# An edge stage whose sums are added by TensorE's identity product and ScalarE's copy instead of VectorE

## The chip, the core and the metric

One NeuronCore of a Trainium2 chip runs one program. The metric is the device time of one execution in microseconds (us). TensorE (PE) multiplies matrices into PSUM, VectorE (DVE) and ScalarE (ACT) work on SBUF and PSUM, GpSimd (POOL) here issues the gathers, SyncE (SP) the plain transfers. Each engine has an instruction stream of its own, handled in order; a wait on a semaphore holds what stands behind it in the same stream.

## The reference

A graph attention layer on 3125 nodes and 53125 edges (sorted by destination) is followed by a mixture of eight experts. Only the attention's edge part matters here:

```
qi = q[dst];  kj = k[src];  vj = v[src]
alpha = sum(qi * kj, -1) / sqrt(D)                 # 4 heads of 64
m     = segment_max(alpha, dst)
ex    = exp(alpha - m[dst])
denom = segment_sum(ex, dst)
out   = segment_sum(ex / denom[dst] * vj, dst)
```

## The kernel before

The program has four stages: `project` (key, value tables), `attend` (the edge stage), `mlp` and `experts`. The change is all in `attend`.

`attend` walks over 232 **steps** (STEPS); a step is 256 edges, two tiles of 128 (LT), that all belong to one block of 128 destination nodes. Eight steps are a **chunk** (CP), four chunks a **round** (CR, RING = 32 steps). `walk` writes the first round out, runs the following ones in a hardware loop, and writes out the rest with the tail of ADD_LAG = 17 places. Every engine has its own `at(i, j)` per place; j is the place in the round.

What a step does, by engine, with j the place:

- POOL (L657) gathers the rows of k and v of both tiles by an indirect DMA each into `ring`. It waits until the product of 8 steps before and the sum of 24 steps before are done.
- PE `expand` (L742) makes the queries of the edges by a one-hot product into one of four `psQ`; it first loads the block's number from `brow` into a register (L738) and waits for the product of four steps before.
- DVE multiplies them with the keys (`prod`, L947), then reduces to `alpha` (L987). Between these two it does the pieces of work named below.
- The running maximum of a whole chunk takes a chain over the next eight steps, one piece per step: `alm` (L868, DVE), two transpositions (L772, L773, PE), a copy `nrow` (L707, ACT), a scan (L873, DVE), then pieces that go to and fro between PE (`psR`, `psM`: L778, L781, L786, L789, L794, L798) and DVE (L877 to L931). PE's piece j stands in `rest`, behind the sum of the same `rest`. In step 6 ACT computes the weights `exp` into `ring` (L713).
- PV: 14 steps behind (PV_LAG), ACT multiplies the values by the weights in place: 2 tiles x 4 heads = 8 ACTIVATEs of 128x64 (L722). In the tail, from step 232 on, `shared` is true: ACT does tile 0, and DVE tile 1 in one instruction of 128x256 (L957), with its own semaphore s_pvd.
- DVE makes the one-hot matrix `oh` (L965). 16 steps behind, PE sums with it: four passes of 260 columns into `psA[b % 2]` (L765).
- 17 steps behind, DVE adds `psA` to the block's row of `acc` in SBUF (L981); the block's number comes from `brow` by a register load (L940). Once per chunk DVE first rescales that row by `fac` (L1005); the addition of the chunk's first step waits for it (s_resc).

PE runs `expand(j)` and then `rest(j - 1)`, in which the sum (of step j - 17) comes first and the chain's piece second. ACT's `at` in the order of the code: `idx` for POOL (L685, step 1), chain pieces (L707 in step 0, L710 and L713 in step 6), PV. DVE's: product, chain piece 0, in the tail PV, `oh`, chain piece 1, step 6's build of the one-hot (L834), the addition, chain piece 2, reduction, in step 0 the rescaling.

Of the kernel before, what the change touches and what calls it, by code (L numbers as in the profile page):

```python
# [24 lines left out]
ALU = mybir.AluOpType  # L25
ACT = mybir.ActivationFunctionType
# [6 lines left out]
NB, BP = 25, 128  # L33
# [4 lines left out]
LT = 2  # L38
# [3 lines left out]
STEPS = TILES + NB - 1  # L42
CP = 8
# [3 lines left out]
CR = 4  # L47
RING = CR * CP
R = H * W
HW_ = D + 1  # L50
HALFW = H * HW_
# [3 lines left out]
PV_LAG = CP + 6  # L55
SUM_LAG = CP + 8
# [447 lines left out]
def attend(nc, ctx, io, keep):  # L504

    c = ExitStack()
    with c:
# [82 lines left out]
        def live(i, j, fresh, lag=0):  # L590

            if fresh:
                return j >= lag
            return not isinstance(i, int) or RING * i + j - lag < STEPS

        def staged(i, j, fresh):

            return live(i, j - j % CP, fresh, CP)

        def shared(i, j):  # L600

            return isinstance(i, int) and RING * i + j >= STEPS

        @block.sync
        def _(sp):
# [59 lines left out]
        @block.scalar  # L665
        def _(act):
            def project_out(t):

                act.wait_ge(s_qp, t + 1)
                if t >= 2:  # L670
                    act.wait_ge(s_qlo, t - 1)
                    act.wait_ge(s_reso[t % 2], 16 * (t // 2))
                nc.scalar.activation(qst[:, t % 2, :], psA[t % NA][:, :], ACT.Copy).then_inc(s_qres, 1)
                act.wait_ge(s_qres, t + 1)
                nc.scalar.activation(q3[:, 0, t, :], qst[:, t % 2, 0:HID], ACT.Copy).then_inc(s_qhi, 1)
                nc.scalar.activation(acc[:, t, 0:HID].rearrange("p (k n) -> p k n", k=KC),
                                     iotaF[:, :].unsqueeze(1).broadcast_to([P, KC, P]), ACT.Copy, scale=0.0).then_inc(s_zero, 1)
                act.wait_ge(s_qr1, t + 1)
                nc.scalar.activation(q3[:, 1, t, :], qst[:, t % 2, 0:HID], ACT.Copy).then_inc(s_qmid, 1)

            def places(cc, par, fresh):

                if not fresh:
                    act.wait_ge(s_kv[CP - 1], 16 * LT * (cc - 1))
                nc.scalar.activation(idx[:, par, :], keep["srcI"][:, bass.ds(W * cc, W)], ACT.Copy).then_inc(s_idx, 1)  # L685

            def starts(m, par):

                nc.scalar.activation(stc[:, par, :, :], keep["startN"][:, bass.ds(W * m, W)].unsqueeze(1).broadcast_to([P, H, W]),
                                     ACT.Copy).then_inc(s_stc, 1)  # L690

            places(0, 0, True)
            for t in range(QEARLY):
                project_out(t)

            def at(i, j, fresh):
                if j % CP == 1 and live(i, j - 1, fresh, -CP):
                    places(CR * i + j // CP + 1, (j // CP + 1) % 2, fresh and j < CP)
                if fresh and QEARLY + j < NB:
                    project_out(QEARLY + j)  # L700
                m = CR * i + j // CP - 1
                jj = j % CP
                if staged(i, j, fresh):
                    if jj == 0:
                        starts(m, (j // CP - 1) % 2)
                        act.wait_ge(s_mp, NT * m + T_IN)
                        nc.scalar.activation(nrow[:, 0:P], psM[0:R, P:2 * P], ACT.Copy).then_inc(s_nrow, 1)  # L707
                    if jj == 6:
                        act.wait_ge(s_mv, NV * m + V_FMIN)
                        nc.scalar.activation(fx[:, :], fm[:, :], ACT.Exp, scale=SCALE).then_inc(s_fx, 1)  # L710
                        act.wait_ge(s_mv, NV * m + V_DIFF)
                        out = ring[:, :, (j // CP - 1) % CR, :].rearrange("p w (h e) -> p h w e", h=H)[:, :, :, D]
                        nc.scalar.activation(out, dif[:, :, :], ACT.Exp, scale=SCALE).then_inc(s_exp, 1)  # L713
                if live(i, j, fresh, PV_LAG):

                    sj = (j - PV_LAG) % RING
                    bc = CR * i + (j - PV_LAG) // CP
                    act.wait_ge(s_exp, bc + 1)
                    for k in range(LT if shared(i, j) is False else 1):
                        for h in range(H):  # L720
                            row = ring[:, LT * (sj % CP) + k, sj // CP, h * HW_:(h + 1) * HW_]
                            last = nc.scalar.activation(row[:, 0:D], row[:, 0:D], ACT.Copy, scale=row[:, D:HW_])  # L722
                    last.then_inc(s_pv, 1)

            walk(act, at)

        @block.tensor
        def _(pe):
# [18 lines left out]
            def rest(i, j, fresh):  # L747
# [4 lines left out]
                if live(i, j, fresh, SUM_LAG):  # L752

                    b = RING * i + j - SUM_LAG
                    sj = (j - SUM_LAG) % RING
                    pe.wait_ge(s_pv, b + 1)
                    if isinstance(b, int) and b >= STEPS - PV_LAG:
                        pe.wait_ge(s_pvd, b - (STEPS - PV_LAG) + 1)
                    pe.wait_ge(s_oh, b + 1)
                    if fresh and j == SUM_LAG:  # L760
                        pe.wait_ge(s_qres, NB)
                    if not (fresh and j < SUM_LAG + NA):
                        pe.wait_ge(s_acc, b - NA + 1)
                    for k in range(LT):
                        last = nc.tensor.matmul(psA[sj % NA][0:BP, 0:HALFW], oh[:, sj % NO, k, :],  # L765
                                                ring[:, LT * (sj % CP) + k, sj // CP, :], start=(k == 0), stop=(k == LT - 1))
                    last.then_inc(s_agg, 1)
                if jj == 0:
                    pe.wait_ge(s_mv, NV * m + V_ALPHA)
                    pe.wait_ge(s_stc, m + 1)  # L770
# [54 lines left out]
        def _(dve):  # L825
# [108 lines left out]
            def at(i, j, fresh):  # L934
                step = RING * i + j
                cc, q, jj = CR * i + j // CP, j // CP, j % CP
                now = staged(i, j, fresh)
                if live(i, j, fresh, ADD_LAG):
                    b = step - ADD_LAG
                    blk = nc.vector.value_load(brow[0:1, bass.ds(b, 1)], min_val=0, max_val=NB - 1)  # L940
                if live(i, j, fresh):

                    dve.wait_ge(s_kv[jj], 16 * LT * (cc + 1))
# [25 lines left out]
                    maximum(i, j, 1)  # L969
                if jj == 6 and live(i, j, fresh, -CP):  # L970
                    build(2 * i + (q + 1) // 2, cc + 1, (q + 1) % CR)
                if live(i, j, fresh, ADD_LAG):

                    sj = (j - ADD_LAG) % RING
                    dve.wait_ge(s_agg, b + 1)
                    if not (fresh and j < ADD_LAG + 1):
                        dve.wait_ge(s_acc, b)
                    if sj % CP == 0:
                        dve.wait_ge(s_resc, CR * i + (j - ADD_LAG) // CP + 1)
                    row = acc[:, bass.ds(blk, 1), :].rearrange("p a d -> p (a d)")  # L980
                    nc.vector.tensor_tensor(row, row, psA[sj % NA][0:BP, 0:HALFW], ALU.add).then_inc(s_acc, 1)  # L981
                if now:
                    maximum(i, j, 2)
                if live(i, j, fresh):
# [837 lines left out]
```

## Time and profile before

| | us |
|---|---|
| median of three runs | 1486.68 (1482.07 to 1489.24) |
| the profiled execution | 1487.41, span 1485.6 |
| PE, DVE, ACT, POOL busy | 1259.2, 1099.3, 780.8, 836.5 |
| last addition of the edge stage | at 752 |

The granted TensorE clock is 0.96 on average. Busy time counts neither waits nor the sequencers' register loads. In the timelines a start and a length stand first; lengths overlap, so what an instruction costs is read from start to start. "[0.30 <-issue]" is idle time just before, with what ended it; "issue" is idle time for which the profile shows no other engine's work.

### The profile page before, as it was taken

Reading aid. Unit: us, or ns where it says so; the run is one execution under the profiler, and the core shown is the slowest. Engines: PE = TensorE matmul, PEld = TensorE weight load, DVE = VectorE, ACT = ScalarE, POOL = GpSimd, SP = SyncE. Lnnn points to the kernel's source line nnn. Section 1 sums busy time; section 2 is a strip of 40 time slices with the busy share of each in tenths; the row PEclk is TensorE's granted clock in tenths of the full one; section 3 lists DMA queues with packets and bytes.
Section 4 is the critical chain, followed back from the end, with each engine's and each line's share of the span. In section 5 each row is a group of like instructions: output and inputs, shape, how many; then the busy total and the mean of one; then the engine's idle time right before and its main releaser. Section 6 shows DMA issues by size and latency. Waiting matters only on the chain. (4 is left out here: it accounts for less than half of the span.)

```text
span 1485.6 us, 29780 instructions
## 1 busy us (share of the span) xinstructions
PE 1259.2 (85%) x7188; PEld 985.3 (66%) x7189; DVE 1099.3 (74%) x2825; ACT 780.8 (53%) x2538; POOL 836.5 (56%) x874
## 2 busy tenths in 40 slices
PE   4899877777877777677759999868899999999998
PEld 2434555454555545455537777667899999999997
DVE  4747899898998989899955555367856656566565
ACT  1255888786876778677732222233334434444343
POOL 2146677777777777777310111036566757566564
PEclk9999999999999999999979999968999999999999
DMA  5367777777777777777340111142110010100000
GB/s 186 124 219 221 211 226 224 223 225 222 217 226 226 223 217 225 229 223 220 109 131 4 51 53 53 33 139 65 40 37 19 1 53 0 35 18 0 18 1 17
DMA packets 83555, 184.24 MB, mean 124 GB/s; under 512 B 11611, under 2 KB 46262, under 8 KB 83454
## 3 DMA queue, kind: packets, MB, share of 16 engines
q0 software_dynamic: 37632, 124.28, 29.4%
q1 hardware_dynamic: 44438, 57.57, 11.9%
q10 hardware_dynamic: 1384, 1.32, 0.3%
q8 instruction: 31, 0.51, 0.1%
q14 instruction: 70, 0.57, 0.1%
HBM read 165.93 MB, written 17.18 MB: 123 GB/s over the span
## 5 line engine op out<-in xcount | busy, mean ns | idle before, releaser
L657 POOL DMA_INDIRECT ring<-kv_rows,idx x464 | 478.7, 1032 | 174.7 <-issue 132.3
L722 ACT ACTIVATE ring<-ring 128x64 f32<-128x64 f32 x1800 | 438.3, 336 | 0.9
L1540 ACT ACTIVATE hf<-psF,k_scT 128x320 f32<-128x320 f32 x320 | 197.8, 618 | 221.4 <-PE psF L1573 212.2
L742 PE MATMUL psQ<-k_q,ohT 128*128 x1392 | 206.1, 282 | 93.5 <-issue 93.4
L765 PE MATMUL psA<-ring,oh 128*128 128x260 f32 x928 | 251.4, 395 | 2.7 <-DVE k_acc L981 2.5
L742 PEld LDWEIGHTS psQ<-k_q,ohT 128*128 128x128 bf16 x1392 | 120.5, 98 | 150.3 <-issue 125.8
L1507 POOL TENSOR_TENSOR h2l<-hf,h2h 128x320 fp32r<-128x320 f32 x160 | 148.8, 944 | 111.6 <-DVE h2h L1716 111.6
L947 DVE TENSOR_TENSOR prod<-psQ,ring 128x512 f32<-128x512 f32 x232 | 158.1, 681 | 35.0 <-issue 21.2
L1507 POOL TENSOR_TENSOR h1l<-hf,h1h 128x320 fp32r<-128x320 f32 x160 | 148.5, 950 | 61.5 <-DVE h1h L1716 61.5
L765 PEld LDWEIGHTS psA<-ring,oh 128*128 128x128 f32 x928 | 163.8, 197 | 24.2 <-ACT ring L722 4.1
L987 DVE TENSOR_REDUCE alpha<-prod 128x8 f32<-128x512 f32 x232 | 155.8, 671 | 0.2
L1716 DVE CAST h2h<-hf 128x320 fp32r<-128x320 f32 x160 | 89.8, 577 | 63.3 <-ACT hf L1540 63.3
L1716 DVE CAST h1h<-hf 128x320 fp32r<-128x320 f32 x160 | 82.5, 521 | 58.5 <-ACT hf L1540 58.4
L1573 PE MATMUL psO<-wh,h2l 128*128 128x256 f32 x400 | 108.8, 293 | 9.1 <-DVE o L1705 8.3
L1705 DVE SCALAR_TENSOR_TENSOR o<-psO,wt,o 128x256 f32<-128x256 f32 x200 | 92.5, 479 | 30.7 <-PE psO L1573 29.2
L1573 PE MATMUL psO<-wl,h2h 128*128 128x256 f32 x400 | 105.6, 285 | 0.0
L1573 PE MATMUL psF<-xh,wl 128*128 128x320 f32 x320 | 101.3, 324 | 0.0
L1573 PE MATMUL psF<-xl,wh 128*128 128x320 f32 x320 | 100.2, 320 | 0.0
L1573 PE MATMUL psF<-h1h,wl 128*128 128x320 f32 x320 | 97.5, 313 | 0.0
L1573 PE MATMUL psF<-h1l,wh 128*128 128x320 f32 x320 | 96.3, 309 | 0.0
L1137 POOL TENSOR_SCALAR ve<-mv 128x5 f32<-128x5 f32 x10 | 3.3, 329 | 164.2 <-DVE mv L1261 99.5
L981 DVE TENSOR_TENSOR k_acc<-k_acc,psA 128x260 f32 x232 | 93.7, 404 | 2.8 <-PE psA L765 1.0
(234 smaller groups left out, 2323.6 us busy)
## 6 DMA issues: line engine op xcount, KB each, us to landing
ohT<-step_destinations SPq DMA_DIRECT2D x29, 512.0 KB, 5.0
ring<-kv_rows,idx POOLq DMA_INDIRECT x464, 3.8
kv_rows<-kvst SPq DMA_DIRECT2D x25, 260.0 KB, 2.1
we<-in_L_ffn_W SPq DMA_DIRECT2D x16, 256.0 KB, 3.1
residual<-qst SPq DMA_DIRECT2D x25, 128.0 KB, 3.5
resin<-residual SPq DMA_DIRECT2D x5, 640.0 KB, 6.6
after_graph_layer<-x SPq DMA_DIRECT2D x5, 640.0 KB, 5.7
xres<-after_graph_layer SPq DMA_DIRECT2D x5, 640.0 KB, 4.4
```

The costliest lines, as they stand in the source:

```text
L657: nc.gpsimd.indirect_dma_start(out=ring[:, LT * (j % CP) + k, j // CP:j // CP + 2, :].rearrange("p t e -> p (t e)"), out_offset=None, in_= ...
L722: last = nc.scalar.activation(row[:, 0:D], row[:, 0:D], ACT.Copy, scale=row[:, D:HW_])
L742: last = nc.tensor.matmul(psQ[j % NQ][:, k * HID:(k + 1) * HID], ohT[par][:, w * P:(w + 1) * P], q3[:, part, bass.ds(blk, 1), :].rearrange ...
L765: last = nc.tensor.matmul(psA[sj % NA][0:BP, 0:HALFW], oh[:, sj % NO, k, :], ring[:, LT * (sj % CP) + k, sj // CP, :], start=(k == 0), sto ...
L947: nc.vector.tensor_tensor(prod[:, j % 2, :].rearrange("p (k d) -> p k d", k=LT), psQ[j % NQ][:, :].rearrange("p (k d) -> p k d", k=LT), ri ...
L981: nc.vector.tensor_tensor(row, row, psA[sj % NA][0:BP, 0:HALFW], ALU.add).then_inc(s_acc, 1)
L987: nc.vector.tensor_reduce(alpha[:, q % 2, :, LT * jj:LT * jj + LT].rearrange("p h w -> p w h"), prod[:, j % 2, :].rearrange("p (k h d) -> ...
L1507: nc.gpsimd.tensor_tensor(low, hf[:, n, 0:b - a], high, ALU.subtract).then_inc(s_rl, 1)
L1540: nc.scalar.activation(hf[:, n, 0:b - a], psF[n][:, 0:b - a], ACT.Relu, bias=scT[:, 2 * layer - 1, col + m:col + m + 1], scale=scT[:, 2 * ...
L1573: mm = nc.tensor.matmul(out, ws(k)[iw], xs(k)[ix], start=(at == 0), stop=(at == len(n) - 1))
L1705: nc.vector.scalar_tensor_tensor(out=o[:, u, :], in0=ps, scalar=wt[:, u, e:e + 1], in1=o[:, u, :], op0=ALU.mult, op1=ALU.add).then_inc(s_c ...
L1716: nc.vector.tensor_copy(high, hf[:, n, 0:b - a]).then_inc(s_rh, 1)
```

## The change

In every step, not only in the tail, `shared` is now true in odd places and false in even ones: in odd ones DVE scales tile 1 and ACT tile 0, in even ones ACT scales both. The addition leaves DVE. PE gets, behind the sum, a register load of the block's number, a wait for the copy of the step before (and, in a chunk's first step, for the rescaling), and a product of the identity with the block's row of `acc`, accumulated into the same `psA`. ACT gets a register load and a copy of `psA` into that row of `acc`, ahead of its chain pieces and PV.

```diff
         def shared(i, j):
-            return isinstance(i, int) and RING * i + j >= STEPS
+            return j % 2 == 1
...
         (ACT, at)
+                if live(i, j, fresh, ADD_LAG):
+                    b = RING * i + j - ADD_LAG
+                    blk = nc.scalar.value_load(brow[0:1, bass.ds(b, 1)], min_val=0, max_val=NB - 1)
+                    act.wait_ge(s_agg, b + 1)
+                    nc.scalar.activation(acc[:, bass.ds(blk, 1), :].rearrange("p a d -> p (a d)"),
+                                         psA[(j - ADD_LAG) % RING % NA][0:BP, 0:HALFW], ACT.Copy).then_inc(s_acc, 1)
...
-                    for k in range(LT if shared(i, j) is False else 1):
+                    for k in range(LT if not shared(i, j) else 1):
...
         (PE, rest)
-                    if isinstance(b, int) and b >= STEPS - PV_LAG:
-                        pe.wait_ge(s_pvd, b - (STEPS - PV_LAG) + 1)
+                    if sj % 2 == (1 - PV_LAG) % 2:
+                        pe.wait_ge(s_pvd, (RING // 2) * i + (j - SUM_LAG) // 2 + 1)
...
                     for k in range(LT):
-                        last = nc.tensor.matmul(psA[sj % NA][0:BP, 0:HALFW], oh[:, sj % NO, k, :],
-                                                ring[:, LT * (sj % CP) + k, sj // CP, :], start=(k == 0), stop=(k == LT - 1))
-                    last.then_inc(s_agg, 1)
+                        nc.tensor.matmul(psA[sj % NA][0:BP, 0:HALFW], oh[:, sj % NO, k, :],
+                                         ring[:, LT * (sj % CP) + k, sj // CP, :], start=(k == 0), stop=False)
+                    blk = nc.tensor.value_load(brow[0:1, bass.ds(b, 1)], min_val=0, max_val=NB - 1)
+                    if not (fresh and j < SUM_LAG + 1):
+                        pe.wait_ge(s_acc, b)
+                    if sj % CP == 0:
+                        pe.wait_ge(s_resc, CR * i + (j - SUM_LAG) // CP + 1)
+                    nc.tensor.matmul(psA[sj % NA][0:BP, 0:HALFW], ident[:, :], acc[:, bass.ds(blk, 1), :].rearrange("p a d -> p (a d)"),
+                                     start=False, stop=True).then_inc(s_agg, 1)
...
         (DVE, at)
-                if live(i, j, fresh, ADD_LAG):
-                    b = step - ADD_LAG
-                    blk = nc.vector.value_load(brow[0:1, bass.ds(b, 1)], min_val=0, max_val=NB - 1)
...
-                if live(i, j, fresh, ADD_LAG):
-
-                    sj = (j - ADD_LAG) % RING
-                    dve.wait_ge(s_agg, b + 1)
-                    if not (fresh and j < ADD_LAG + 1):
-                        dve.wait_ge(s_acc, b)
-                    if sj % CP == 0:
-                        dve.wait_ge(s_resc, CR * i + (j - ADD_LAG) // CP + 1)
-                    row = acc[:, bass.ds(blk, 1), :].rearrange("p a d -> p (a d)")
-                    nc.vector.tensor_tensor(row, row, psA[sj % NA][0:BP, 0:HALFW], ALU.add).then_inc(s_acc, 1)
```

## Rows read from the trace of the kernel before

**Rows 1.** Stretches: start:end, us, busy us (instructions) by engine, clock, DMA share, GB/s.

```profile
185.00:722.00 537.00, 407.79 (x2363) 277.12 (x2361) 498.15 (x1374) 418.05 (x1760) 415.06 (x400) 0.97 0.77 223
```

**Rows 2.** Groups from 185 to 722: line, engine, op, tiles | busy us, mean ns | idle before.

```profile
L657 POOL DMA_INDIRECT ring<-kv_rows,idx x400 | 415.1, 1038 | 121.8 <-issue 96.6 <-PE psA L765 17.4 <-DVE prod L947 6.7
...
L742 PE MATMUL psQ<-k_q,ohT 128*128 x1220 | 180.9, 282 | 89.4 <-issue 89.3
```

**Rows 3.** Timeline of POOL: start us, length us, line, op [idle before].

```profile
409.26 0.95 POOL L657 DMA_INDIRECT ring<-kv_rows,idx  x1 [0.30 <-issue]
...
414.25 1.22 POOL L657 DMA_INDIRECT ring<-kv_rows,idx  x1 [0.30 <-DVE prod L947]
...
422.03 1.66 POOL L657 DMA_INDIRECT ring<-kv_rows,idx  x1 [0.30 <-DVE prod L947]
```

**Rows 4.** Timeline of DVE, step 7 of two rounds, and the loop's end.

```profile
363.27 0.68 DVE L947 TENSOR_TENSOR prod<-psQ,ring 128x512 f32<-128x512 f32 x1
...
449.20 0.69 DVE L947 TENSOR_TENSOR prod<-psQ,ring 128x512 f32<-128x512 f32 x1
...
455.03 0.69 DVE L947 TENSOR_TENSOR prod<-psQ,ring 128x512 f32<-128x512 f32 x1 [3.75 <-issue]
```

**Rows 5.** Timeline of all engines, steps 7, 0 and 1 around a rescaling.

```profile
406.80 0.69 DVE L947 TENSOR_TENSOR prod<-psQ,ring 128x512 f32<-128x512 f32 x1
407.12 0.74 PEld L765 LDWEIGHTS psA<-ring,oh 128*128 128x128 f32 x4
...
407.89 0.75 PEld L742 LDWEIGHTS psQ<-k_q,ohT 128*128 128x128 bf16 x6
...
409.54 0.42 DVE L965 TENSOR_TENSOR oh<-k_iotaF,k_dstR 128x256 f32<-128x256 f32 x1
...
409.77 0.27 PE L772 MATMUL psM<-k_ident,alm 128*64 128x128 f32 x1
...
410.18 0.27 ACT L707 ACTIVATE nrow<-psM 64x128 f32<-64x128 f32 x1 [1.07 <-PE psM L773]
...
410.80 0.42 DVE L1005 TENSOR_TENSOR k_acc<-k_acc,fac 128x260 f32 x1
...
411.39 1.04 PE L765 MATMUL psA<-ring,oh 128*128 128x260 f32 x4
...
411.95 0.40 DVE L873 TENSOR_TENSOR_SCAN F<-nrow,psM 64x128 f32<-64x128 f32 x1
...
412.59 0.41 DVE L981 TENSOR_TENSOR k_acc<-k_acc,psA 128x260 f32 x1
412.92 0.67 DVE L987 TENSOR_REDUCE alpha<-prod 128x8 f32<-128x512 f32 x1
```

**Rows 6.** Timeline of DVE one chunk on, steps 7 and 0.

```profile
426.73 0.69 DVE L947 TENSOR_TENSOR prod<-psQ,ring 128x512 f32<-128x512 f32 x1
...
431.16 0.69 DVE L947 TENSOR_TENSOR prod<-psQ,ring 128x512 f32<-128x512 f32 x1 [2.35 <-DMA ring<-kv_rows,idx]
```

**Rows 7.** Groups of the whole span: the scaling on DVE, copies from PSUM, the sum.

```profile
L957 DVE TENSOR_TENSOR ring<-ring 128x256 f32<-128x256 f32 x14 | 5.8, 413 | 0.7 <-ACT ring L713 0.4 <-issue 0.2
...
L254 ACT ACTIVATE k_acc<-psT 128x256 f32<-128x256 f32 x25 | 9.6, 383 | 61.2 <-PE psT L285 61.2
...
L673 ACT ACTIVATE qst<-psA 128x512 f32<-128x512 f32 x25 | 14.9, 595 | 17.2 <-PE psA L806 16.4 <-DMA residual<-qst 0.7
...
L765 PE MATMUL psA<-ring,oh 128*128 128x260 f32 x928 | 251.4, 395 | 2.7 <-DVE k_acc L981 2.5
```

**Rows 8.** Timeline of ACT in the tail.

```profile
740.40 7.74 ACT L722 ACTIVATE ring<-ring 128x64 f32<-128x64 f32 x32
```

**Rows 9.** Instructions of line L738: duration ns min/median/max.

```profile
L738 PEldq TENSOR_LOAD <-k_brow x203: 296/302/322, 186.6 to 720.8; - x102
```

**Rows 10.** Timeline of PE: a chunk product and the expansion behind it.

```profile
403.15 0.27 PE L794 MATMUL psM<-k_ident,Gm 64*128 64x64 f32 x1
404.05 0.85 PE L742 MATMUL psQ<-k_q,ohT 128*128 x6 [0.63 <-issue]
```

## The prediction

> **What bounds the kernel now.** I read the table of stretches first: the edge stage is the only one that the change touches, and in its steady part (185 to 722 us) VectorE (DVE) is busy 93% of the time, TensorE (PE) 76%, ScalarE (ACT) 78%, GpSimd (POOL) 77% [rows 1]. That invites "DVE is the bound, take work off it". The list of groups says more: POOL's 400 gathers there take 1038 ns each and each is preceded by 0.30 us of idle time, so 400 x 1.342 = 537 us, the whole stretch of 537 us [rows 2]. The timeline of POOL shows it as a chain without a hole: every gather starts 0.30 us after the one before, and what stretches it is that some last 1.14 to 1.66 us instead of 0.95 [rows 3]. A step has two gathers, so a round of 32 steps costs 64 x 1.342 = 85.9 us, and DVE's product of step 7 of a round's last chunk stands at 363.27 and, one round on, at 449.20: 85.9 us [rows 4].
>
> DVE's own pace is faster. From a chunk's product of step 7 at 406.80 to the next at 426.73 are 19.9 us, in a dense row [rows 5, 6]. Four chunks are 79.7 us; at the loop's end DVE loses 3.75 us before its next product [rows 4]; together 83.5 us. The 2.4 us to 85.9 are waits for a gather: "2.35 <-DMA" before the product at 431.16 [rows 6]. So a round has two limits, 85.9 by the gathers and 83.5 by the chain of DVE and PE, and the change works on the second alone. **Making DVE lighter cannot pay more than the gathers allow**; making the chain longer costs from 2.4 us per round on.
>
> **What leaves and what comes, per chunk of 8 steps.** DVE loses eight additions of 0.41 us; by starts they cost 0.33 each (412.59 to 412.92) [rows 5]. It gains four scalings of 128x256; the tail has this instruction 14 times, 0.413 us each [rows 7], so by the same overlap 0.33. Net 8 x 0.33 - 4 x 0.33 = -1.3 us: DVE alone would need 18.6. Its register load for the addition goes too; it lay under the reduction and is worth 0 to 0.1 us each.
>
> ACT loses 16 of 64 scalings per chunk, 0.24 us each by starts (7.74/32) [rows 8], -3.9, and gains eight copies of 128x260 out of PSUM. No such copy is in the trace; 128x256 from PSUM takes 383 ns [rows 7], so 8 x 0.4 = +3.2, up to 0.6 each at the upper end (128x512 takes 595 ns) [rows 7]. ACT is busy 78% and stays there. But its copy stands first in its step, and now two engines wait for it.
>
> PE gains a product of 260 columns in two passes per step. Four such passes take 1.04 us with the overhang of the last, whose own length is 0.39, so they start (1.04 - 0.39)/3 = 0.22 apart [rows 5, 7]: +0.44 us. It also gains a register load. The one that is there shows 302 ns for the load alone [rows 9]; by starts a chunk's product at 403.15 is followed by the expansion at 404.05, 0.9 us later, though where PE had queued work, as behind the sum at 407.12, the expansion's weights load at 407.89 with no gap [rows 5, 10]. The new load stands behind four queued passes (0.88 us), so I take it as hidden, with 0.9 us per step as the other end. The price of a step in PE's instruction stream is then: expansion to sum 0.6, sum 0.88, identity 0.44, chunk product 0.3, and 0.2 of the next register load left over: 2.4 us. DVE's step is 18.6/8 = 2.3. So **PE becomes about equal to DVE, and each wait in front of it counts**.
>
> **The new waits.** PE's product for step b now waits for ACT's copy of b-1, and on the first step of a chunk for DVE's rescaling. What is queued behind it on PE is the scan's transposition of that same slot, and behind that is ACT and DVE. Three stalls per chunk follow. I place them from X, the end of the rescaling (411.22) [rows 5].
>
> First: the transpositions of alm and stc ran at 409.77, before the rescaling, and ACT's nrow was done at 410.45, 0.8 before. Now they stand behind the identity product that waits for X: X + 0.1 + 0.5 (identity) + 0.45 (two transpositions) + 0.3 (nrow) gives the scan at X + 1.45. It ran at 411.95, X + 0.73. Stall 0.7.
>
> Second: ACT's queue has nrow, then the eight scalings of that even step (1.9 us), then the idx copy (0.1), then the copy of the sum. Nrow is done at X + 1.35, so the copy is seen at X + 3.8; PE's next identity product waits for it, and the carry product behind it is done at X + 4.8. DVE would want that (L877) at X + 1.45 + 3 x 0.33 (scan, scaling, one-hot) + 2 x 0.6 (reduction, next product) = X + 3.65. Stall 1.2.
>
> Third: PE's following step starts late for the same reason, and DVE's read of cin meets its product 0.4 late. After that both run at 2.3 to 2.4 and meet again at the next rescaling. Sum: 19.9 - 1.3 + 0.7 + 1.2 + 0.4 = 20.9 us per chunk.
>
> A round: 4 x 20.9 + 3.75 = 87.4 us against 85.9 now, +1.5. With 232/32 = 7.25 rounds, +11 us. Bounds of the stalls: none (the round stays at 85.9, +0), and twice as long (+2.3 per chunk, 96.6 per round, +77); I take the placed ones, since each is a queue order read from the code with durations from rows.
>
> **The tail.** From step 232 on DVE has scaled one tile of two in each step already; now ACT takes both in even steps. The last eight such steps cost ACT 7.74 us for 32 scalings without a gap, 0.97 per step [rows 8]; after, (48 x 0.24 + 8 x 0.4)/8 = 1.84. That is 0.87 more for each of the seven or so steps in which no scan gives it cover: about +6, between +2 and +10. The stages before and after are untouched.
>
> **Sum.** The profiled execution took 1487.4 us (span 1485.6), 0.7 above the median of 1486.7. 1487.4 + 11 + 6 = 1504.4; I say 1505.
>
> **A rule on the port.** Gathers that run beside a DVE instruction with two SBUF inputs (L965 at 409.54) last the usual 0.95 us (the one of 409.26) [rows 3, 5]; the new scaling is of that kind and adds no lengthening by this row. The Trainium skill (SBUF — State Buffer, "SBUF: two separate sides") says that DVE and GpSimd take a shared pair of ports by exclusive lock, in a fast mode of DVE or, against a GpSimd instruction that reads SBUF, with two SBUF inputs, and that GpSimd then cannot write descriptors. By that rule this trace agrees only if a gather does not count as reading SBUF. If it does count, it would speak against this change, and the time is that of the third rival.
>
> **The rivals.**
> 1. The gathers still decide. If the three stalls sum to under about 1.9 us instead of 2.3, the round stays under 85.9: 1487.4 + 0 + 2 to 6 = 1489 to 1494. For: the difference is only 0.4 us in a chunk. Against: the queue orders are strict.
> 2. PE's stream decides. If the new register load is not hidden for 0.3 us or so of each step, PE needs 2.7 per step, a chunk 21.6 plus part of the stalls, some 22: 4 x 22 + 3.75 = 91.8, +5.9 per round, +43, with the tail 1536. At the full 0.9 it would be 3.3 per step, 26 per chunk, +166; the gap-free expansion at 407.89 speaks against that. For: the idle time before expansions, 89 us, is called "issue" [rows 2], so the sequencer does cost time there. It decides from 2.6 us per step on.
> 3. The gathers get longer. Each of 116 new DVE scalings holds a gather back for up to 0.41 us: 16 x 0.41 = 6.6 per round on 85.9, 92.5 per round, +48 at most; half of it 1487 + 24 + 6 = 1517. For: the gathers' lengths do vary, 1038 ns mean over the usual 0.95 us. Against: L965 above.
> 4. Faster. If DVE's lighter load let gathers run at the shortest length, 64 x 1.25 = 80 per round, and the stalls hid, 4 x 18.6 + 3.75 = 78, the round could fall to 80: -5.9 x 7.25 = -43, with the tail 1450; a third of it, some 1478, is likelier. It needs both at once. Nothing on DVE that is removed is known to lengthen a gather.
>
> **How the numbers follow.** The forecast 0.45, own range 1495 to 1520; rival 1 0.22; rival 2 0.20; rival 3 0.05; rival 4 0.08. Half a per cent, 7.4 us, is about what a measurement can tell from no change. Slower by over that: all of 2 and 3, nearly all of the forecast, a little of 1: 0.70. Same: 0.22. Faster: 0.08. The range leaves out rival 4 and the long end of rival 2: 1486 to 1545.
>
> **What would show it.** In the profile after: POOL has waits longer than 0.30 us before its gathers (now it has none), and a round is over 86 us; DVE waits some 0.7 us before L873 on ACT's nrow and 1.2 us before L877 on PE, once per chunk; ACT idles before its copies, waiting for PE; expansions are not over 2.5 us apart outside these places. If POOL still has no hole, rival 1 holds; if PE is never idle but for "issue" and steps are 2.6 or more throughout, rival 2; if gathers' mean is over 1100 ns, rival 3. Wrong altogether would be a stage under 85 us per round.

## The result, and the profile after

The changed kernel takes 1520.16 us (1519.73 to 1527.88), the kernel before in the same comparison 1485.85 (1481.53 to 1489.24): ratio 1.0238, 95% interval 1.0216 to 1.0261. Slower, as forecast, and inside the range; but +34 us by the medians where +18 was forecast, and at the upper end of the 1495 to 1520 that the prediction gave its own mechanism. The profiled execution is the longest of its six, 1527.88 (span 1526.1).

First the stretch of [rows 1] in the kernel after (same columns), then POOL's gathers from 190 to 734 us (in [rows 2] they are those from 185 to 722):

```profile
185.00:722.00 537.00, 472.60 (x2637) 330.69 (x2635) 450.86 (x1209) 372.04 (x1481) 419.27 (x382) 0.98 0.75 214
```

```profile
L657 POOL DMA_INDIRECT ring<-kv_rows,idx x386 | 425.3, 1102 | 119.0 <-issue 99.0 <-PE psA L779 11.3 <-DVE prod L957 4.4
```

DVE is busy 84% of the stretch instead of 93%, ACT 69% instead of 78%, PE 88% instead of 76%: two engines were relieved and the stage got slower. Only 382 gathers fit where 400 did, and they last 1102 ns on average instead of 1038.

What DVE waits for, in the kernel after, 190 to 734 us (us in total, times, longest):

```profile
DVE tails L890 <- PE psR L791: 27.2, 25, 1.8
DVE F L886 <- ACT nrow L714: 23.9, 24, 1.6
DVE prod L957 <- PE psQ L749: 11.9, 4, 3.1
DVE cin L902 <- PE psR L794: 9.6, 22, 0.5
...
DVE prod L957 <- DMA ring<-kv_rows,idx: 0.4, 1, 0.4
```

And the same list for the kernel before, 190 to 707 us:

```profile
DVE prod L947 <- issue: 21.0, 10, 4.1
DVE prod L947 <- DMA ring<-kv_rows,idx: 9.0, 7, 2.4
```

The waits for gathers are gone, and three waits have come, each about once per chunk (22 to 25 times): on ACT's `nrow`, on PE's carry product, on PE's product behind `cin`. These are the three places that were forecast. The timeline of the kernel after around one rescaling shows how the first two come about (start, length, engine, line, idle before):

```profile
427.40 0.43 DVE L1005 TENSOR_TENSOR k_acc<-k_acc,fac 128x260 f32 x1 [0.34 <-issue]
...
428.08 0.70 PE L779 MATMUL psA<-k_acc,k_ident 128*128 x2 [0.29 <-DVE k_acc L1005]
...
428.62 0.27 PE L785 MATMUL psM<-k_ident,alm 128*64 128x128 f32 x1
...
429.04 0.27 ACT L714 ACTIVATE nrow<-psM 64x128 f32<-64x128 f32 x1 [2.39 <-PE psM L786]
...
429.21 2.01 ACT L729 ACTIVATE ring<-ring 128x64 f32<-128x64 f32 x8
429.41 0.41 DVE L886 TENSOR_TENSOR_SCAN F<-nrow,psM 64x128 f32<-64x128 f32 x1 [0.97 <-ACT nrow L714]
...
431.23 0.36 ACT L708 ACTIVATE k_acc<-psA 128x260 f32 x1
...
431.73 0.70 PE L779 MATMUL psA<-k_acc,k_ident 128*128 x2 [0.76 <-ACT k_acc L708]
...
432.37 0.27 PE L791 MATMUL psR<-k_ident,F 64*1 64x64 f32 x2
...
432.67 0.21 DVE L890 COPY tails<-psR 1x64 f32<-1x64 f32 x1 [1.01 <-PE psR L791]
```

The identity product (L779) waits for the rescaling; the transposition L785 stands behind it, `nrow` behind that, and DVE's scan comes 1.6 us after the rescaling's end, where it came 0.7 after it in [rows 5]. Then ACT does eight scalings before its copy (431.23), PE's next identity product waits for the copy, the carry product (L791) stands behind it, and DVE waits 1.01 us.

Where the time lies, from the starts of DVE's products and of the gathers:

| us | before | after | |
|---|---|---|---|
| to the first gather | 88.4 | 91.4 | +3.0 |
| first gather to product of step 31 | 109.3 | 110.5 | +1.2 |
| six rounds, product of step 31 to that of step 223 | 509.0 | 532.1 | +23.1 |
| to the last product (step 231) | 19.4 | 22.8 | +3.4 |
| tail: last product to the first use of the sums | 26.7 | 33.3 | +6.6 |
| rest of the program | 732.7 | 735.9 | +3.2 |

The first and the last line are untouched code; from kernel to kernel of this document the first moves between 88.4 and 91.4 us and the last between 729 and 736, without a change in them, so those 6 us are no part of the change. The stage itself gained 34.3 us in this execution. That it equals the difference of the medians is chance: the profiled executions lie 40.5 us apart, and how much of the 34.3 a median execution has isn't known.

### The profile page after: what moved, and what is told of

Its sections match the earlier page's. It is cut to its first block and busy times, and to the rows that moved or that the text cites. A ratio compares the mean times of both kernels' runs of the same rounds, so it can differ in the third digit from the quotient of the medians.

```text
span 1526.1 us, 31630 instructions
## 1 busy us (share of the span) xinstructions
PE 1362.9 (89%) x7652; PEld 1069.2 (70%) x7653; DVE 1066.3 (70%) x2695; ACT 763.3 (50%) x2363; POOL 861.0 (56%) x874
## 5 line engine op out<-in xcount | busy, mean ns | idle before, releaser
L657 POOL DMA_INDIRECT ring<-kv_rows,idx x464 | 503.4, 1085 | 177.3 <-issue 138.8
L729 ACT ACTIVATE ring<-ring 128x64 f32<-128x64 f32 x1392 | 355.3, 337 | 0.9
L772 PE MATMUL psA<-ring,oh 128*128 128x260 f32 x928 | 247.5, 390 | 1.0 <-ACT ring L729 1.0
L749 PE MATMUL psQ<-k_q,ohT 128*128 x1392 | 201.7, 280 | 37.1 <-issue 35.5
L779 PE MATMUL psA<-k_acc,k_ident 128*128 x464 | 146.4, 398 | 39.1 <-ACT k_acc L708 19.5
L772 PEld LDWEIGHTS psA<-ring,oh 128*128 128x128 f32 x928 | 161.9, 194 | 19.9 <-ACT ring L729 1.4
L708 ACT ACTIVATE k_acc<-psA 128x260 f32 x232 | 88.5, 381 | 121.3 <-PE psA L779 98.9
L779 PEld LDWEIGHTS psA<-k_acc,k_ident 128*128 128x128 f32 x464 | 82.6, 192 | 73.3 <-issue 61.1
L1705 DVE SCALAR_TENSOR_TENSOR o<-psO,wt,o 128x256 f32<-128x256 f32 x200 | 92.5, 479 | 33.3 <-PE psO L1573 31.9
```

The costliest lines, as they stand in the source:

```text
L657: nc.gpsimd.indirect_dma_start(out=ring[:, LT * (j % CP) + k, j // CP:j // CP + 2, :].rearrange("p t e -> p (t e)"), out_offset=None, in_= ...
L749: last = nc.tensor.matmul(psQ[j % NQ][:, k * HID:(k + 1) * HID], ohT[par][:, w * P:(w + 1) * P], q3[:, part, bass.ds(blk, 1), :].rearrange ...
L779: nc.tensor.matmul(psA[sj % NA][0:BP, 0:HALFW], ident[:, :], acc[:, bass.ds(blk, 1), :].rearrange("p a d -> p (a d)"), start=False, stop=T ...
L1705: nc.vector.scalar_tensor_tensor(out=o[:, u, :], in0=ps, scalar=wt[:, u, e:e + 1], in1=o[:, u, :], op0=ALU.mult, op1=ALU.add).then_inc(s_c ...
```

## The experiments

In all of them the six rounds of the table serve as the measure of the stage. e1 to e4 ran on one chip (kernel before 1483.6 us), e5 and e10 to e12 on a second (1482.39), e6 to e9 on a third, of which more below. "After the first" means the last five of the six rounds; the first of them has no end of the hardware loop in it.

**What the gathers allow in the kernel before.** DVE's addition shrunk to 4 of 260 columns (the kernel leaves out the rest of the sums):

```diff
-  nc.vector.tensor_tensor(row, row, psA[sj % NA][0:BP, 0:HALFW], ALU.add)
+  nc.vector.tensor_tensor(row[:, 0:4], row[:, 0:4], psA[sj % NA][0:BP, 0:4], ALU.add)
```

> The kernel before, with DVE's additions cut to 4 of 260 columns (the other columns of the sums are left out); waits and order are unchanged. It asks whether the gathers limit the kernel before. If they do (my theory): DVE's own chunk falls from 19.9 to some 18 us, but a round stays near 85.9 us and the time within 1472 to 1486. Rival, that a gather's shown length is only what the chain of DVE and PE leaves it: a round falls by some 8 to 10 us and the time to 1415 to 1430.

1472.92 us, ratio 0.9907 (0.9872 to 0.9942); six rounds 496.6. The waits and the gathers, 190 to 720 us:

```profile
DVE prod L947 <- DMA ring<-kv_rows,idx: 16.8, 20, 2.4
...
L657 POOL DMA_INDIRECT ring<-kv_rows,idx x397 | 397.4, 1001 | 120.9 <-issue 105.4 <-PE psA L765 8.8 <-DVE prod L947 5.8
```

In the stretch of [rows 1] DVE is busy 467.76 us instead of 498.15. With rounds of 83.6 and 85.8 us that is 72.8 us per round instead of 79.6, 6.8 less; but a round after the first became only 2.2 us shorter, and the waits for gathers grew (16.8 us where the kernel before has 9.0): they are a limit of the kernel before, as expected. But the limit itself moved, from 1038 to 1001 ns a gather. 64 x (1.001 + 0.305) = 83.6 us is the round that it had (82.8 to 85.0 after the first).

**The additions alone.** The whole change but for `shared`, so that ACT scales all tiles except in the tail:

```diff
-  return j % 2 == 1
+  return isinstance(i, int) and RING * i + j >= STEPS
```

> The other half: the additions go to PE and ACT, ACT scales all tiles but in the tail. DVE needs 8 x 0.33 = 2.6 us less per chunk than before, 17.3, with the stalls of 2.8 us 20.1; but ACT has 8 x (8 x 0.24 + 0.4) = 18.6 us per chunk in a loop with PE, and its backlog behind nrow is longer. My theory: 21 to 22.5 us per chunk, 1512 to 1540. Rival, that the extra scaling on DVE and not the copy on ACT makes the changed kernel slow: under 1500.

1502.48 us, 1.0118 (1.0081 to 1.0156); six rounds 520.5. Waits and gathers, 190 to 720 us:

```profile
DVE tails L890 <- PE psR L791: 34.3, 24, 2.0
DVE F L886 <- ACT nrow L714: 25.6, 24, 1.6
DVE prod L957 <- issue: 22.3, 5, 5.1
DVE cin L902 <- PE psR L794: 9.4, 23, 0.5
...
L657 POOL DMA_INDIRECT ring<-kv_rows,idx x392 | 384.2, 980 | 147.3 <-issue 117.5 <-PE psA L779 24.9 <-DVE prod L957 4.0
```

The three waits are there, 69.3 us in 24 chunks, 2.9 per chunk; the gathers are short, and POOL has idle time of 0.376 us before one instead of 0.305: here they wait, and the chain sets the pace. The time lies between the two expectations: the three waits are there, but moving the additions carries only half of the loss.

**The DVE scaling alone.** Kernel before with `shared` as after; the additions stay on DVE.

```diff
-  return isinstance(i, int) and RING * i + j >= STEPS
+  return j % 2 == 1
```

> The kernel before with one half of the change: DVE scales one of four value tiles, the additions stay on DVE. DVE gets 4 x 0.33 = 1.3 us per chunk more. With the gathers' limit of 85.9 us: a round is 4 x 21.2 + 3.75 = 88.6, +2.7, in all with 2 to 3 us for the tail 1504 to 1512. Without such a limit 29 x 1.3 = +38: 1522 to 1526. If the ports are contended, the gathers' mean goes over 1100 ns and DVE waits for them.

1525.76 us, 1.0273 (1.0234 to 1.0312), no better than the whole change, whose interval it overlaps. It is above the 1504 to 1512 expected with a limit by the gathers and in the 1522 to 1526 expected without one; DVE has no wait for a gather that shows. Its six rounds, 543.5, are 11 us longer than those of the whole change. A chunk takes 21.4 us (median), 1.5 more than the 19.9 before: four scalings of 0.37. That gives 4 x 21.4 + 3.75 = 89.4 per round, but a round after the first took 91.0 to 91.9. The missing 2 us stand at the loop's end, timeline of DVE:

```profile
474.28 0.69 DVE L947 TENSOR_TENSOR prod<-psQ,ring 128x512 f32<-128x512 f32 x1 [4.07 <-issue]
...
476.86 0.43 DVE L981 TENSOR_TENSOR k_acc<-k_acc,psA 128x260 f32 x1 [1.43 <-issue]
```

A second gap, before the addition two instructions on, was not there before; the profile calls it "issue" too. What makes it was not found.

**The order on PE.** In three kernels PE's pieces of the scan were put ahead of the sum and the identity product: with the whole change only the two transpositions (e2), with the whole change all pieces (e11), with the additions alone all pieces (e10). The edit in each is a move inside `rest`:

```diff
+                if jj == 0:
+                    ...                    # transpositions of alm and stc
+                if jj == 2:
+                    ...                    # carry product and the later pieces, in e10 and e11
                 if live(i, j, fresh, SUM_LAG):
                     ...                    # sum and identity product
-                if jj == 0:
-                    ...
```

> The changed kernel, with PE's two transpositions of a chunk's step 0 ahead of the sum and the identity product instead of behind them. It takes away the cause of the first stall (nrow waits behind the rescaling) and, since ACT's eight scalings and its copy then start earlier, of the second. My theory: DVE's waits before L886 and before L890, 0.97 and 1.08 us per chunk in the changed kernel, go nearly to zero, a chunk falls from 21.4 to 19.4 to 19.9 us, and the gathers' 85.9 us per round then limit: 1495 to 1506. Without a limit by the gathers it would be 1460 to 1470. Rival, that PE's instruction stream is the bound: 1515 to 1520, no change.

> The whole change with the same order on PE: scan pieces ahead of the sum and the identity product in every step. Theory (the gathers, lengthened by the DVE scaling to 1065 to 1085 ns, then decide): DVE no longer waits before the scan and the tails, the round is 64 x (1.07 + 0.304) = 87.9, as it was with only the transpositions moved: 1503 to 1512. Rival (the DVE scaling does not lengthen gathers, they only follow the chain's pace): they fall back to 1000 to 1040 ns and the round to 83.5 to 86, time 1478 to 1495.

> Additions alone moved (ACT scales as before), and PE's pieces of the scan (transpositions, carry product) stand ahead of the sum and the identity product in every step. With the additions moved and no DVE scaling the gathers lasted 980 ns, so their limit is 64 x (0.980 + 0.304) = 82.2 us per round against 85.9 before. Theory (only the three placed waits held that version back): they go, the chunk falls from 20.8 to 19 to 19.8 us, the round to 80 to 83.5, and the time to 1468 to 1488 with a tail 6 us longer, ratio 0.99 to 1.003. Rival (PE's stream is the next limit once the waits are gone): the chunk stays at 20.3 or over, round 85 to 87, time 1488 to 1500.

| | median us | ratio (95%) | six rounds |
|---|---|---|---|
| whole change | 1520.16 | 1.0238 (1.0216 to 1.0261) | 532.1 |
| e2, transpositions first | 1507.86 | 1.0151 (1.0109 to 1.0193) | 521.5 |
| e11, all pieces first | 1507.81 | 1.0159 (1.0110 to 1.0208) | 521.0 |
| e4, additions alone | 1502.48 | 1.0118 (1.0081 to 1.0156) | 520.5 |
| e10, additions alone, all pieces first | 1489.16 | 1.0024 (0.9998 to 1.0049) | 504.7 |
| kernel before | | | 509.0 |

e10's waits of DVE and its gathers, then those of e11, then e2's, 190 to 720 us:

```profile
DVE prod L957 <- PE psQ L749: 51.7, 75, 3.9
DVE prod L957 <- issue: 22.0, 7, 5.2
...
L657 POOL DMA_INDIRECT ring<-kv_rows,idx x397 | 393.4, 991 | 129.8 <-issue 95.2 <-PE psA L810 19.2 <-DVE prod L957 12.9
```

```profile
DVE prod L957 <- PE psQ L749: 50.2, 80, 3.8
DVE k_acc L1005 <- ACT k_acc L708: 9.6, 24, 1.3
...
L657 POOL DMA_INDIRECT ring<-kv_rows,idx x385 | 413.4, 1074 | 117.3 <-issue 96.0 <-PE psA L810 10.7 <-DVE prod L957 7.3
```

```profile
DVE prod L957 <- DMA ring<-kv_rows,idx: 18.3, 14, 2.9
DVE tails L890 <- PE psR L791: 17.8, 22, 1.6
DVE prod L957 <- PE psQ L749: 14.8, 14, 3.0
...
L657 POOL DMA_INDIRECT ring<-kv_rows,idx x384 | 413.5, 1077 | 117.0 <-issue 93.3 <-PE psA L786 17.4 <-DVE prod L957 5.5
```

The waits before the scan, the tails and `cin` are all gone from e10 and e11, and with them 15.8 and 11.1 us of the six rounds: the queue order on PE was the cause of them, shown in both pairs (each pair lies on two chips, whose kernels before agree within 0.3%). With the transpositions alone ahead, e2, the first of the waits goes and the second stays at 17.8 us of 27.2, where nearly nothing was expected. What is late next differs. In e10 it is PE's expansion (51.7 us in 75 waits): PE's stream is the limit, at 84.1 us per round, between the two expectations, and the time is the kernel before's. In e2 it is the gathers again (18.3 us), with 64 x (1.077 + 0.305) = 88.4 us per round against 88.0 seen after the first. e11 has the same gathers, 64 x (1.074 + 0.305) = 88.3, and 87.5 seen, but DVE's waits there are for PE's expansion (50.2 us) and 1.3 us in all for gathers: PE's stream holds it, at about the gathers' own pace.

The four kernels make a square. Pieces behind instead of ahead: +0.9 points of the ratio without the scaling, +0.8 with it. Scaling on DVE: +1.4 with pieces ahead, +1.2 behind. Each ratio is known to 0.2 to 0.5 points. So of the loss of 2.4 points **about a third (0.8 to 0.9 points) is the order on PE and about half (1.2 to 1.4) the scaling on DVE**, as long as the additions are moved. Where they stay on DVE the same scaling costs 2.7 points (e3, against 2.4 for both): moving the additions costs 1.2 by itself and nothing that shows beside the scaling, so the costs of the two edits don't add up. What is left, e10's 0.2, is no more than a measurement can tell from nothing, and is made of 4 us less in the rounds and 5 us more in the tail (32.0 against 26.7).

**Does the register load on PE cost?** The whole change, the identity product reading row 0 always, without the load of the block's number:

```diff
-  blk = nc.tensor.value_load(brow[0:1, bass.ds(b, 1)], min_val=0, max_val=NB - 1)
...
-  nc.tensor.matmul(..., ident[:, :], acc[:, bass.ds(blk, 1), :].rearrange("p a d -> p (a d)"), ...)
+  nc.tensor.matmul(..., ident[:, :], acc[:, 0, :], ...)
```

> The whole change, but PE's identity product reads row 0 of the accumulator always, so that PE loads no register for it (the sums are then wrong, the work is the same otherwise). Theory (the placed waits and the longer gathers make the time): the register load lay under queued passes, the chunk stays at 21 to 21.5 us, the round at 88 to 89.5, the time within 6 us of the whole change's 1520, ratio to before 1.019 to 1.025. Rival (PE's instruction stream costs): 0.3 us or more of each step comes back, the chunk falls by 1.5 to 2.4 us, the round falls to the gathers' own limit of 87 to 88 us, and the time to 1500 to 1508, ratio 1.010 to 1.015.

1515.11 us, 1.0198 (1.0147 to 1.0249); six rounds 529.3 against 532.1, 0.5 us per round. Its interval takes in the whole change's ratio: 2.8 us in 192 steps, 0.015 a step. The gathers hide a part of it: a chunk without a loop's end fell from 21.4 to 21.1 us, 0.04 a step, while DVE now waits for gathers, 190 to 720 us:

```profile
DVE prod L956 <- DMA ring<-kv_rows,idx: 2.5, 4, 1.4
```

Either way the load is nearly hidden, and the prediction's second rival, which needed 0.3 a step, is out.

**What a DVE instruction does to the gathers.** The additions alone, plus a product of 128x256 on DVE in odd steps, into a tile that nobody reads:

```diff
+  if j % 2 == 1:
+      nc.vector.tensor_tensor(scr[:, :], ring[:, LT * jj, q + 1, 0:HID],
+                              ring[:, LT * jj + 1, q + 1, 0:HID], ALU.mult)
```

> Additions alone moved, as in the version that took 1502, plus a product of two 128x256 SBUF tiles on DVE in odd steps, where the change has its scaling; its result goes to a scratch tile that nobody reads, and nobody waits for it. The chunk gets 4 x 0.33 to 4 x 0.41 = 1.3 to 1.6 us of DVE's time. Theory (any such instruction on DVE lengthens the gathers beside it): gathers' mean goes from 980 to 1030 or more, and the time from 1502 to 1515 to 1530, ratio 1.020 to 1.030. Rival (the lengthening in the whole change came through ACT or PE, not through DVE's product): gathers stay within 15 ns of 980, and the time rises only by DVE's own share, 4 x 1.3 to 1.6 per round in the chain or +35 at most, with the gathers' waits for free slots growing instead.

1507.98 us, 1.0152 (1.0097 to 1.0207), six rounds 522.9. Its gathers, 190 to 720 us:

```profile
L658 POOL DMA_INDIRECT ring<-kv_rows,idx x388 | 406.9, 1049 | 123.9 <-issue 96.6 <-PE psA L780 25.2 <-ACT idx L686 1.8
```

1049 ns against 980 in e4, and 991 in e10 on the same chip: with a DVE instruction more, on which nothing depends, the gathers get longer; the work of ACT and PE is the same as in e4. Not because the dummy stands beside them, though. In the six rounds the gathers exceed 946 ns (their median) by 39 us in all instead of 12 in e4, and 18 of these 27 us fall on one gather per chunk, the one under way when DVE builds `ohT` in step 6, an even step, in which the dummy doesn't run. The dummy moves what DVE does against the gathers; the section on the hardware has the rows.

The time rose by 5 us only, less than the 13 to 28 expected, and by ratio not clear of noise (1.0152 against e4's 1.0118). DVE's waits took up most of the new work (before the scan 16.5 us instead of 25.6, before `cin` none instead of 9.4), and the longer gathers were not yet the limit. The real scaling costs some 18 us. It has the dummy's length on DVE, but PE's sum waits for the scaled tile, and ACT scales less; which of these makes the difference no run shows.

**On the third chip** the same kernels e10, e11 and e12 had run before (as e7, e6, e8), and e9, in which one input of the dummy product comes from PSUM:

```diff
-  nc.vector.tensor_tensor(scr[:, :], ring[:, LT * jj, q + 1, 0:HID],
+  nc.vector.tensor_tensor(scr[:, :], psQ[j % NQ][:, 0:HID],
```

> The changed kernel with all of PE's chain pieces (not only step 0's) ahead of the sum and the identity product of the same place. My theory: DVE's waits before L886, L890 and L902 come from the order on PE, so they fall below 0.3 us per chunk together; DVE's own chunk is then under 19.5 us, and what limits is the gathers, which DVE's scaling lengthens (1071 ns mean with the transpositions first): 64 x (1.07 + 0.30) = 88 us per round, 1500 to 1508. Rival, that PE's instruction stream with its second register load is the bound: 1515 or more, and expansions 2.6 us or more apart.

> The additions moved alone (ACT scales all tiles, as in e4_adds_alone), with PE's chain pieces ahead of the sum in every place. If the stalls of e4 (35.5, 26.6 and 9.6 us of DVE waits) come from the order on PE and the gathers keep their 980 ns without DVE's scaling, a round falls from 87.5 us to the gathers' 64 x 1.284 = 82.2 or to ACT's 4 x 19.5 = 78 plus the loop's end: 1460 to 1480, faster than the kernel before. If ACT's eight scalings behind nrow are the cause of the second wait, L890's wait stays and it is 1490 to 1500.

> e4_adds_alone with one added DVE instruction in odd places, a product of 128x256 of two tiles in SBUF (both in the gathered ring) into a scratch tile that nobody reads. It has the size and the two SBUF inputs of the scaling. If such an instruction holds gathers back, their mean rises from 980 by 50 to 120 ns; if it does not, it stays within 15 ns. Either way DVE's chain gets 4 x 0.33 = 1.3 us per chunk longer: 1520 to 1542 against 1502.

> The same as e8_two_sbuf, but the added instruction reads one tile in PSUM and one in SBUF. If two SBUF inputs are what lengthens gathers, the mean stays within 15 ns of 980 here while it rises in e8; if any DVE time of that length does it, both rise alike. The time is that of e8 or, if gathers matter to it, less: 1515 to 1540.

There the kernel before takes 1647.33 us and a round of e7 109.8 us after the first (84.7 in e10), so that the expected times don't apply; the gathers, 64 x 1.31 = 84 us a round, don't limit it there. The ratios are 1.0169 (1.0109 to 1.0228) for e6, 1.0079 (1.0045 to 1.0114) for e7, 1.0259 (1.0201 to 1.0317) for e8 and 1.0280 (1.0209 to 1.0352) for e9. e6 and e7 keep the order that e11 and e10 have on the second chip, but e8 is e12's kernel, which had 1.0152 there: ratios don't carry over from chip to chip. e8 and e9 are alike in time. The gathers of e8, e9 and, without a dummy, e7, 190 to 720 us:

```profile
L658 POOL DMA_INDIRECT ring<-kv_rows,idx x302 | 317.0, 1050 | 214.1 <-issue 115.5 <-remote 48.9 <-DVE prod L961 26.5
```

```profile
L658 POOL DMA_INDIRECT ring<-kv_rows,idx x302 | 307.7, 1019 | 223.5 <-issue 130.6 <-remote 56.6 <-PE psA L780 31.6
```

```profile
L657 POOL DMA_INDIRECT ring<-kv_rows,idx x310 | 311.7, 1006 | 219.5 <-issue 72.1 <-remote 63.1 <-PE psA L810 62.3
```

With one input in PSUM the gathers last 1019 ns, with both in SBUF 1050, without a dummy 1006; over the whole stage the means are 1028, 1035 and 1004. So the dummy with one PSUM input adds 13 or 24 ns, the one with two SBUF inputs 44 or 31, by the stretch that is taken: a mean over gathers doesn't settle whether the inputs matter (e7 also has the other order on PE, which goes with 11 ns between e4 and e10). The Trainium skill (SBUF — State Buffer, "SBUF: two separate sides") has GpSimd locked out of a port pair shared with DVE. That gathers end at fixed distances behind one DVE instruction, as the last section shows, agrees with it; which of DVE's instructions lock and why there are two distances no run here tells.

## Why the prediction was right, and where its sizes were not

- *The gathers bound the kernel before, the chain the kernel after.* Right: e1 for the first; for the second, 0.4 us of waits for gathers in the kernel after, and 11 us less when the order on PE alone is changed (e11).
- *Three stalls of 0.7, 1.2 and 0.4 us per chunk.* Right in place and sum: 23.9/24 = 1.0, 27.2/25 = 1.1 and 9.6/22 = 0.4, 2.5 against 2.3.
- *DVE needs 18.6 us without the stalls.* The chunk is 21.4 us in the median, without 2.5 that is 18.9. So a chunk was 0.5 us longer than forecast and a round 2.0.
- *A round of 87.4.* Measured 88.7 to 89.8 from the second on, 89.2 on average; 4 x 21.4 + 3.0 = 88.6. The loop's end is now a gap of 2.90 to 3.31 us, put down to PE's expansion in four of five, instead of 3.55 to 4.12 of issue.
- *+1.5 per round, times 7.25.* This is the term that was mis-sized: 11 us forecast, 27.7 measured to the last product, made of +1.2 before the six rounds, +6.2 in the first of them, +3.4 in each of the other five, and +3.4 in the last chunk. The kernel before ran that first round in 79.8 us, faster than the gathers' 85.9 and without a loop's end, on rows gathered ahead: POOL had issued the last gather of a step 18 us before its product at the stage's start, 12 us at the start of this round and 6 us at its end. A lead is spent before the gathers decide, and until then the chain's full price shows. The forecast put 85.9 under every round. That the time fell into the stated range owes something to luck: the range reached up to 1545 for the second rival, whose register load e5 finds nearly hidden, and so a loss nearly twice the forecast's still lay in it.
- *The tail, +6.* Right: +6.6. As forecast, ACT sets it: it takes 1.77 us per step there against 0.97 of [rows 8] and 1.84 forecast; the copy lasts 381 ns where 0.4 us was taken. Timeline of ACT in the tail after:

```profile
765.11 2.01 ACT L729 ACTIVATE ring<-ring 128x64 f32<-128x64 f32 x8
767.02 0.37 ACT L708 ACTIVATE k_acc<-psA 128x260 f32 x1
767.29 1.05 ACT L729 ACTIVATE ring<-ring 128x64 f32<-128x64 f32 x4
768.36 0.39 ACT L708 ACTIVATE k_acc<-psA 128x260 f32 x1
768.64 2.01 ACT L729 ACTIVATE ring<-ring 128x64 f32<-128x64 f32 x8
```

- *The sign POOL would give.* Wrong: 0.308 us before a gather, no hole, though the gathers aren't the limit. They became longer, 64 x (1.102 + 0.308) = 90.2 us per round, more than the chain's 89, and lived off their lead: POOL's instruction for the last gather of a step ended 13.3 us before the product of step 64, and 12.2, 10.5, 9.6, 7.2 and 2.4 us before those of steps 96, 128, 160, 192 and 224. With more rounds, by these numbers, they would have decided again. By the prediction's own signs the first rival (no hole in POOL) and the third (a mean over 1100 ns) had come true; the third's price was hidden under the chain's. The argument against it, that the gather beside L965 lasts 0.95 us, was one row. In the kernel before's six rounds the 219 gathers in whose first 0.95 us L965 runs last 1092 ns on average, the other 165 last 970.
- *The share of the two edits.* By the prediction's terms a chunk without the scaling needs 20.9 - 1.3 = 19.6 us and a round 4 x 19.6 + 3.75 = 82.2, under the gathers' 85.9, so that moving the additions alone would cost only the tail, some 6 us. e4 measured a chunk of 20.6 us (median without the loop's ends) and 18.9 us in all. The scaling on top was worth the 11 us of the rounds; it costs 1.2 to 1.4 points, 18 to 20 us.
- *The fourth rival's clause, that nothing removed from DVE is known to lengthen a gather.* The additions are such a thing: with small ones (e1) the mean fell from 1038 to 1001 ns, without them (e4) to 980.

## What to carry to other kernels

An engine that is 93% busy isn't relieved by putting its work into a chain of two others: the identity product and the copy made every step's sum wait for the step before across two engines, and whatever stood behind them in the same streams (here the scan's pieces) waited too; moving those pieces ahead took away about a third of the loss with no other edit. Compare the two limits of a stage, chain and gathers, with the lead that one has over the other: while it lasts, the idle time in front of the slower one tells nothing. No version tried here that does all the work beats the kernel before.

## What the runs showed of the hardware

- The mean length of a gather moves with what DVE has to do: 980 ns with neither additions nor scaling, 1001 with tiny additions, 1038 with additions, 1049 with a dummy product and no additions, 1081 with both additions and scaling, 1074 to 1102 with scaling and no additions. The amount of DVE's work doesn't set it: e2, e11 and the whole change have the same of it, and 1077, 1074 and 1102 ns, and the kernel before, where DVE is busier than in these (498 us of the stretch of [rows 1] against 451 in the kernel after), has 1038.
- The mean hides two kinds of gather. In every kernel here the median is 946 to 949 ns; over 1000 ns last 93 of the 384 in the six rounds of the kernel before, 144 in the kernel after, 50 in e4. Where a gather is under way when DVE's build of `ohT` (L834 before, L847 after) ends, it ends 0.13 or 0.82 us behind that end. Two cases of the kernel after, then one of the kernel before (start, length):

```profile
311.06 1.36 POOL L657 DMA_INDIRECT ring<-kv_rows,idx  x1 [0.30 <-issue]
311.56 0.73 DVE L847 TENSOR_SCALAR ohT<-ohT,k_iotaP 128x2048 bf16<-128x2048 bf16 x1
332.43 2.06 POOL L657 DMA_INDIRECT ring<-kv_rows,idx  x1 [0.30 <-issue]
332.94 0.73 DVE L847 TENSOR_SCALAR ohT<-ohT,k_iotaP 128x2048 bf16<-128x2048 bf16 x1
```

```profile
424.83 0.74 DVE L834 TENSOR_SCALAR ohT<-ohT,k_iotaP 128x2048 bf16<-128x2048 bf16 x1
425.24 1.15 POOL L657 DMA_INDIRECT ring<-kv_rows,idx  x1 [0.30 <-issue]
```

All 24 such gathers of the six rounds do so in the kernel before (15 at 0.125 to 0.128 us, 9 at 0.824 to 0.827) and in the kernel after (7 and 17), and nearly all do in the other kernels, with lengths from 1.02 to 2.07 us. That is how a gather would end that is held until the instruction is over, and its length would then depend on where in it the instruction falls, not on how much DVE does. These 24 last 1491 ns on average before, 1817 after, 2032 in e11. The other gathers average 1009, 1050 and 1006 ns, so this one instruction makes a part of the means, and not all of it.
- One chip of the three runs the kernel before in 1647 us instead of 1483. By e7 all of the extra time is in the edge stage: the rest of the program takes 734.4 us there. DVE, in e8 there, has waits whose releaser the profile calls "remote", and no list shown from the other two has one. What they are was not found.

```profile
DVE tails L891 <- PE psR L792: 30.8, 19, 2.0
DVE cin L903 <- remote: 24.0, 10, 3.7
...
DVE scr L959 <- remote: 19.0, 7, 4.8
```
